# A two-layer decoder on one core: the first self attention's scores on sixteen 32x32 parts of the array, masks without scores, and a new order of steps

## The chip, the core and the metric

The kernel runs on one core of a Trainium2 chip. The core has a matrix engine (PE, with its weight loads shown apart as PEld), a vector engine (DVE), a scalar engine (ACT), a general engine (POOL) and a queue for transfers (SP). The metric is the device time of one execution in microseconds; the median of several runs is given. Traces come from one profiled execution.

## The reference

Sixteen sequences `x` of 128 tokens by 128 features pass through six residual stages; `ctx` is a context of the same shape.

```python
x = x + L0_attn(layernorm(x))          # self0: causal, 16 heads of 8
x = x + L0_xattn(layernorm(x), ctx)    # cross0: 8 heads of 64
x = x + L0_ffn(layernorm(x))           # ffn: ternary weights, rounded activations
x = x + L1_attn(layernorm(x))          # self1: causal, 16 heads of 8, scores clipped at +-10
x = x + L1_xattn(layernorm(x), ctx)    # cross1: 16 heads of 64
x = x + L1_ffn(layernorm(x))           # moe: 8 gated experts
# L0_attn, per head h:
scores = einsum('bhqd,bhkd->bhqk', q, k) * scale
scores = where(key > query, -inf, scores)
attn = softmax(scores)                 # then attn @ v and the output projection
```

## The kernel before, in words

Each sequence is one tile of 128 partitions by 128 columns. A stage is cut into steps, named stage.step: for self0 these are `rs`, `nm`, `xT`, `xTe` (layer norm and turning over), `qk`, `qke` (projection and its copies), `v`, `ve`, `vc` (values, cut in three bf16 parts), `s1` (scores), `mx.0`, `mx.1` (DVE: row maximum and difference, of eight heads each), `t.0`, `t.1` (PE: turning the differences over), `ex` (ACT: exponentials), `lo` (POOL: low part of the weights), `pv`, `at`, `oT`, `oTe`, `y`, `res`. Each step runs once for each of the sixteen sequences, written below as s1(3) for sequence 3. The keys and values of the context (`cross0.k`, `cross1.v` and so on) don't depend on `x` and are made ahead. The steps named `hi` and `lo` of a weight (`e_k.hi` on ACT, `e_k.lo` and `m_w.lo` on POOL) cut it once into a high and a low part.

`ORDER` (line 209) holds one string for each engine: two letters for a step, and the next sequence each time the step comes again. Every engine runs its string as written, and waits on semaphores where a step needs another engine's. The `Plan` class walks the strings with the durations given in `all_steps` (line 82, the entry of `self0.s1` is on line 114) and picks PSUM banks; the banks of two heads' groups (S) are pairs of the eight banks, the smaller fills (X) take one.

`self0.s1` (line 1217) makes the scores of all 16 heads in four PSUM banks, four heads to a bank. Partition is the query, column is head and key. First it writes the causal mask, -1e30 where key > query, with 16 bf16 matmuls on 32x32 parts of the array (line 1228): stationary a 32x32 part of an identity, moving a mask tile repeated over four heads, 512 columns. The four mask tiles hold the mask with its rows turned by 0, 32, 64 and 96 partitions, so each of the sixteen pairs of row part r and query part b finds its rows. Then `quarters` (line 1240) adds the scores with four fp32 matmuls on 32x128 parts (line 1244): 32 rows (four heads' features) of the queries as stationary, the keys of four heads as moving, each head in its own rows and zeros in the others' (`by_head`). `self1.s2` uses `quarters` alone. Going from one division of the array to another is counted by the plan (`array_parts`, `switch`).

At the end, with no more sequences to fill in, PE runs `keep_busy`: matmuls of a mask that nobody reads, one ahead of the last `moe.g` and four ahead of the last `moe.gT`. After that `moe.gT` turns the gate weights over, ACT copies them (`gTe`), and the last `moe.b` adds parts of the experts and biases.

Of the kernel before, what the change touches and what calls it, by code (L numbers as in the profile page):

```python
# [14 lines left out]
P = 128  # L15
NSEQ = 16
# [65 lines left out]
def all_steps():  # L82
# [22 lines left out]
    def self_attention(L, source, maxima, following, loads, loads_out):  # L105
# [8 lines left out]
        add(f"{L}.{first}", "PE", 1240 if maxima else 875, [f"{L}.qke"], [f"{L}.pv"], "S", turns)  # L114
# [52 lines left out]
    for name, load, engine, hi, lo in (("ctx0", "c0", "DVE", 530, 610), ("b_k", "b_k", "DVE", 530, 610),  # L167
# [42 lines left out]
    PE=(  # L210
        "aHaJa4a4aOa4aLa6a4aHa6aQaJa6aUa6bYbqbWbWbYbWaXaObYaLb2b2aZaUbYb0aHaQaJb0b0b0a1a6aXaObaa4aLaHbcaJaZaQ"
        "bea1aUa6b2a4b0a4aXaObabWaLbjbcaUaHblaZaQaJbebnbWa1aXbYbWaOaZbwa4a1aLa4bab2bcbybjaHaUbeblbCaQbGbEbabn"
        "bYaJaXbcbJaZaLb2bja1bebwblaHa6bya4a6bQaObCa6bEbna6baaUbSbjbcbUbGaQbJblb6bebwb8bybnccb0aXbCcabQaLaJbE"
        "claZaHbGbSbUa1chbjbJcjblb6bacqb8bwcabycccla4bncsbQaOb2bWaJbcbSaQa6bCcubUbEaUchbWbwcvbybeb6cqcaaXbJcs"
        "aZb8aLbGaHcza1clcccja4cCcDcubjcvbQb2aObCaJa4bSblcHbaaUa6czbcbUbEbncCaQchbeb6bGcDbJaXcacLb8cqaLbwcHcl"
        "cjcsccbQcuaZaHbycva1bWbYbSbjbUaOblbaaJbYbCbcaUbEcLczbnaQbWcCcqcDbGchb6bebJcscjbwcaaXb8cHbyclccaZa4a1"
        "bQcua6bjaLaHcvaObCaJblbEb0aQbGbnbaczbSaUcqcCbUbcchbJcsbeaXcLbwb6cDcaaZb8a1bycHclcjccbQbWb2cucLcvbSbj"
        "bUaLaOblbCb0babEbnaQczaHbcbGaUcCcDaJb6cqb8bebJcsaXchcaaLbwcccjaZbyclaHa1cua6cvbja4bQaOblbScHa4aJbnba"
        "aQczbcaUbCcCcqbUbEcDcLchbebJcscjaXb6bGbWb8aZcacHaLa1ccclbwcubyaHcvbjbYbQaOblbSbCb2bUbEbaaQbccLbnchb6"
        "aUczb8bGcCcabebJcjbYcDcqccclcsaXcucHbwcvaZbybQaJbjaLb0b0a1blaObCa6aHbEbna6bSaQcLbYczaJbUbGbaaUcCchcD"  # L220
        "bccqb6bwbebJaXcab8cjcsccaZaLbyclcHcua1aHcvbjbYb0aOblbQb2bnbaaUbcczaQchcCaJcqbSbeaXbUcLcDcscjaOaZb6b0"
        "bCcab8bGa1aLaQbEccaUbwclbjbybYcuaXcvblbJaZb2babncHczbccqa1cCbecsbCcLcDbYbabQbcbGcHchbSbEcLbUbjcjbJbe"
        "blcub6bwcvb8bycabWccczbnclbQcDbjb2bSbWcCbCbUblbEchbncqbJb6cjbwcabGb8byclcscccubQcvb0b2bWbScHbCbWczbw"
        "bEcLbGcCbUchcDbycjbJb6cqb8cacsccclbCcucvbEb0bQbJbGbSbYbUchb2cHczcjb6bYcCcacqb8clcsbQcccLbSb0bUcucDcv"
        "b6b2b8cacqchccczcjclcscCcDcHb2cub0cvchcLcqcjcHczcscCcucLcvcDczcHcCcLcDcHcL"
    ),
    DVE=(
        "aEarataEavaPaEaTaEbpbraYaTaPa2aEaYaPaTbfaEa2bhaYaTaPaEbfboa2aYbubhbxa2aTbzaPbfaEbobhaYbubKbNbfbxa2bz"
        "bhbRaTboaPbVbubKbNbxbfbzbocdbhaYcfbRcmaEbVa2cobubNbKbxbzcdcmbocfbRaPbuaTaEbVcobxcwbzbfaYbKbNbhcmcBa2"
        "cdcEcocGcJcwbRaTcfaPbVcEcBbocGbfaEbubKbNcMcJaEbhbxcmaYcdbRbzcwa2cobVaTaPcfcMcBbocEcGcJbubfbNbKbhbxaY"  # L230
        "bzcmcda2bRcocfcwaPaTboaEcEcBbVbucGbKbNbfaYcMbxcJbha2cmbzcdbRcocMcwcfbVaPaTcBbocEaEcGcJbubfbNbKbhaYbx"
        "cdbzcma2cfcwcobRaPaTbocBcEbVcGcMcJbfbKaEbNaYbhbua2cdbxcmbzcwcfbRaPbVaTboaEcMcocEcBcGbfbNbKbhbucJcdcm"
        "aYbxcwbzbRcfa2coaPboaTbVcMcBcEbucGcJbxbfbNaYbKbhcdbzcma2cwcfcoaTaPbRbocBcEcGbfbVaYcMbucJbhaPaTa2cdbx"
        "cmbzcfaYcwcobKbNbocBa2cEbfcGcMbhbRcJbVbubNbKbfbxcwbzcMbhcdbocBcmbRcfcocEbVcGcJbobubKbNbxbzcmbucdbRcw"
        "cfcocBbxcEcMbVcGcJbzbNbKcdcmcwcfbRbKbVcobNcBcEcGcmbRcdbVcocfcMcwcJcdcBcmcfcEcocwcGcMcJcBcEcGcwcMcJcE"
# [13 lines left out]
        "aRcicFbTcraKbtbgb5ctckbBb7a0b1bDcbbHb9bvaMaRbFaVcebkcna9bZbBbma0cybbb3bLcAbdcIcrbOcFa9bgctbbbZbDbtcI"
        "bHbdbTcibFbkb5ckbObvbLb7bgb9cybmbXcbcAbBcecnbkbTbXbDb3cFbmbFcibtb5crbvb7bLcbbObtb9bHckctcncebvbBb1b3"  # L250
# [1280 lines left out]
```

## Time and profile before

| | us |
|---|---|
| median of 3 runs | 499.54 (499.09 to 501.29) |
| the profiled execution | 499.82 |
| its span, first to last instruction | 498.1 |
| PE busy | 489.5 |
| ACT busy | 436.5 |
| DVE busy | 399.9 |
| POOL busy | 370.7 |

The span lies inside the device time; 1.7 us of the profiled execution lie around it. Busy time is the union of an engine's instructions; the ends of matmuls are modelled, and successive ones overlap, so the distance from start to start says more of PE than the sum of durations.

### The profile page before, as it was taken

What the parts mean: (1) busy time and instruction counts of PE and PEld (TensorE: products, weight loads), DVE (VectorE), ACT (ScalarE), POOL (GpSimd) and SP (SyncE); (2) the same over time, 40 slices, a digit from 0 to 9 for tenths busy, and PEclk for the clock granted to TensorE, in tenths of its full rate; (3) what the DMA queues carried; (4) which work ended last, traced back from release to release, by engine and by line L of the source; (5) the groups of instructions that cost most, each with busy time, mean ns of one, the idle gap of its engine ahead of it and who ended that gap; (6) DMA issues with size and microseconds to landing.
All of it is one profiled execution on the core that took longest, in us unless ns stands there. A gap on an engine that the chain in (4) does not pass through costs nothing.

```text
span 498.1 us, 15720 instructions
## 1 busy us (share of the span) xinstructions
PE 489.5 (98%) x5514; PEld 417.4 (84%) x5514; DVE 399.9 (80%) x906; ACT 436.5 (88%) x1180; POOL 370.7 (74%) x455
## 2 busy tenths in 40 slices
PE   8999999999999999999999999999999999999997
PEld 4778887888888888889889888888888898988885
DVE  5767778897888888989898898878898687866765
ACT  5988889999998898998898898989789899989782
POOL 2876677797868887788768886976869688568754
PEclk9999999999999999999999999999999999999999
DMA  6900000000000000000000000000000000000000
GB/s 194 338 2 1 3 2 2 1 2 2 2 3 1 7 2 9 1 3 7 7 3 1 8 3 5 4 7 1 4 7 1 8 7 3 7 3 2 7 7 16
DMA packets 6460, 8.64 MB, mean 17 GB/s; under 512 B 1392, under 2 KB 4848, under 8 KB 6384
## 3 DMA queue, kind: packets, MB, share of 16 engines
q1 hardware_dynamic: 5952, 6.86, 4.1%
q8 instruction: 45, 0.74, 0.6%
q10 hardware_dynamic: 432, 0.79, 0.4%
q14 instruction: 31, 0.25, 0.2%
HBM read 6.50 MB, written 1.05 MB: 15 GB/s over the span
## 4 chain that ended last, share of the span: by engine, by line
PE 90%; ACT 4%; DVE 2%; SPq 1%; DMA 1%; issue 1%; POOL 1%; DVEq 0%; POOLq 0%; ACTq 0%
PE psum L1270 14%; PE psum L1257 10%; PE psum L1297 10%; PE psum L1213 8%; PE psum L1335 8%; PE psum L1244 6%; PE psum L1283 3%; PE psum L1463 3%; PE psum L1347 3%; PE psum L1308 2%; PE psum L1285 2%; PE psum L1316 2%; PE psum L1310 2%; PE psum L1317 2%; PE psum L1318 2%; PE psum L1309 2%
## 5 line engine op out<-in xcount | busy, mean ns | idle before, releaser
L723 POOL TENSOR_TENSOR w_self<-w_self 128x1024 f16<-128x1024 f32 x64 | 121.1, 1899 | 27.5 <-ACT w_self L794 13.8
L805 ACT ACTIVATE w_cross<-psum,row_max_cross 128x128 f32<-128x128 f32 x384 | 104.1, 408 | 5.6 <-DVE row_max_cross L980 4.6
L728 POOL TENSOR_TENSOR w_cross<-w_cross,e_rec_cross 128x1024 f32<-128x1024 f32 x48 | 90.9, 1897 | 20.6 <-DVE e_rec_cross L989 20.6
L980 DVE TENSOR_REDUCE row_max_cross<-psum 128x8 f32<-128x1024 f32 x48 | 57.9, 1214 | 13.6 <-PE psum L1257 13.0
L987 DVE TENSOR_REDUCE e_sum_cross<-w_cross 128x8 f32<-128x1024 f32 x48 | 58.2, 1213 | 4.4 <-ACT w_cross L805 4.2
L1257 PE MATMUL psum<-kT_cross,qT_cross 64*128 64x128 f32 x768 | 54.4, 283 | 0.0
L1297 PEld LDWEIGHTS psum<-w_cross,v_cross 128*64 128x64 f32 x768 | 41.1, 136 | 14.3 <-issue 11.0
L813 ACT ACTIVATE w_cross<-psum 128x1024 f32<-128x1024 f32 x48 | 49.9, 1042 | 3.4 <-PE psum L1270 3.2
L1257 PEld LDWEIGHTS psum<-kT_cross,qT_cross 64*128 64x128 f32 x768 | 46.3, 187 | 6.8 <-issue 4.9
L1297 PE MATMUL psum<-w_cross,v_cross 128*64 128x128 f32 x768 | 51.4, 278 | 0.3 <-ACT w_cross L813 0.3
L1270 PE MATMUL psum<-ident,w_cross 128*128 128x128 f32 x384 | 49.8, 274 | 0.1
L1270 PEld LDWEIGHTS psum<-ident,w_cross 128*128 128x128 f32 x384 | 43.1, 142 | 1.4 <-ACT by_head_self L770 0.3
L998 DVE TENSOR_TENSOR w_self<-psum,row_max_self 128x1024 f32<-128x1024 f32 x32 | 39.2, 1225 | 2.4
L996 DVE TENSOR_REDUCE row_max_self<-psum 128x8 f32<-128x1024 f32 x32 | 38.9, 1215 | 1.3 <-PE psum L1244 1.0
L1007 DVE SCALAR_TENSOR_TENSOR w_self<-psum,s_bound 128x1024 f32<-128x1024 f32 x32 | 37.8, 1215 | 2.5 <-PE psum L1244 2.4
L788 ACT ACTIVATE w_self<-w_self,shift 128x1024 f32<-128x1024 f32 x32 | 36.9, 1160 | 2.4 <-DVE w_self L1007 2.4
L770 ACT ACTIVATE by_head_self<-psum,head_mask 128x128 f32<-128x128 f32 x128 | 37.2, 403 | 0.0
L794 ACT ACTIVATE w_self<-psum 128x1024 f32<-128x1024 f32 x32 | 33.1, 1035 | 4.1 <-PE psum L1270 3.5
L1244 PE MATMUL psum<-by_head_self,plain_self 32*128 32x512 f32 x256 | 36.5, 639 | 0.2
L770 ACT ACTIVATE attnT_cross<-psum 128x512 f32<-128x512 f32 x48 | 29.7, 621 | 6.9 <-PE psum L1297 6.3
L1335 PE MATMUL psum<-e_o,attnT_cross 128*128 128x128 f32 x256 | 34.3, 277 | 0.0
L1270 PE MATMUL psum<-ident,w_self 128*128 128x128 f32 x256 | 33.5, 274 | 0.4 <-DVE w_self L998 0.4
(213 smaller groups left out, 1377.5 us busy)
## 6 DMA issues: line engine op xcount, KB each, us to landing
out_dram<-x_all SPq DMA_DIRECT2D x16, 64.0 KB, 1.6
x_all<-in_x SPq DMA_DIRECT2D x1, 768.0 KB, 7.6
cT_all<-in_ctx SPq DMA_DIRECT2D x1, 768.0 KB, 9.8
e_k<-in_e_k SPq DMA_DIRECT2D x1, 512.0 KB, 5.4
e_v<-in_e_v SPq DMA_DIRECT2D x1, 512.0 KB, 6.2
e_q<-in_e_q SPq DMA_DIRECT2D x1, 512.0 KB, 8.4
e_o<-in_e_o SPq DMA_DIRECT2D x1, 512.0 KB, 9.6
m_w<-in_m_w SPq DMA_DIRECT2D x1, 512.0 KB, 8.2
```

The lines of the kernel that those rows point to most:

```text
L723: pool.tensor_tensor(L.w_low[u], L.w[u][:], halves(L.w[u][:]), ALU.subtract)\
L728: pool.tensor_tensor(L.diff[u][:].rearrange("p (h k) -> p h k", h=UNIT), L.e[u][:].rearrange("p (h k) -> p h k", h=UNIT), L.e_rec[:, u, :] ...
L770: act.activation(dst, src, ACT.Copy, **scale).then_inc(emptied(i, name)[0], 1)
L805: last = act.activation(L.e[u][:, P * p:P * (p + 1)], S_[:, P * p:P * (p + 1)], ACT.Exp, bias=L.row_max[:, u, p:p + 1])
L813: act.activation(L.w[u][:], group(i, turn)[:], ACT.Copy).then_inc(taken(i, turn)[0], 1)
L980: dve.tensor_reduce(L.row_max[:, u, :], group(i, turn)[:].rearrange("p (h k) -> p h k", h=UNIT), AX_X, ALU.max, negate=True).then_inc(L.ma ...
L987: dve.tensor_reduce(L.e_sum[:, u, :], L.e[u][:].rearrange("p (h k) -> p h k", h=UNIT), AX_X, ALU.add)
L1244: last = pe.matmul(group(i, name, u)[:, 512 * half:512 * (half + 1)], L.plain[rows, :], L.by_head[rows, :, :].rearrange("p j n -> p (j n)" ...
L1257: last = pe.matmul(S_[:, at:at + P], L.qT[rows, h // 2, :], kT[rows, h // 2, i % 2, :], start=True, stop=True)
L1270: last = pe.transpose(S_[:, P * k:P * (k + 1)], L.diff[u][:, P * k:P * (k + 1)], ident[:])
L1297: last = pe.matmul(bank(i, name)[rows, P * pair:P * (pair + 1)], v[:, h, :], L.w[c][:, P * place(h):P * (place(h) + 1)], start=True, stop= ...
L1335: last = pe.matmul(bank(i, y)[:, 0:P], L.attnT[:, k, :], L.o_w[:, k, :], start=k == 0 and not with_x, stop=k == 4 * L.chunks - 1)
```

## The change

The step `self0.s1` makes its scores by 16 fp32 matmuls, one for each pair of row part r (four heads, a bank of its own) and query part b (32 queries), over the keys 0 to 32(b + 1) - 1 of each of its four heads. Keys behind that get the mask alone, by 12 bf16 matmuls (three query parts, four row parts), and the block of 32 keys on the diagonal gets the mask added by 16 more. All of them are on 32x32 parts. `self1.s2` keeps its quarters. The plan's entry for the step goes from 1240 to 980 and the step is taken to leave the array in 32x32 parts. The strings of PE, DVE, ACT and POOL are new orders of the same steps; SP's is the same. The four `keep_busy` matmuls ahead of the last `moe.gT` are gone.

```diff
-        add(f"{L}.{first}", "PE", 1240 if maxima else 875, [f"{L}.qke"], [f"{L}.pv"], "S", turns)
+        add(f"{L}.{first}", "PE", 980 if maxima else 875, [f"{L}.qke"], [f"{L}.pv"], "S", turns)
...
 ORDER = dict(
     PE=(
-        "aHaJa4a4aOa4aLa6a4aHa6aQaJa6aUa6bYbqbWbWbYbWaXaObYaLb2b2aZaUbYb0aHaQaJb0b0b0a1a6aXaObaa4aLaHbcaJaZaQ"
+        "aHaJa4a4aOa4aLa4a6aHaQa6a6a6aUaJbqbYbYbWbWbWaXaObYaLb2aZb2aUb0bYaHaQb0aJa1b0b0a6aXaOaLbaa4aHbcaZaJaQ"
...
     if step == "s1" and L == "self0":
-        return "32 by 32", "32 rows"
+        return "32 by 32", "32 by 32"
...
                     pe.wait_ge(masks_turned, 16 * 6)
-                for j in range(4):
-                    for b in range(4):
-                        queries, r = slice(32 * b, 32 * (b + 1)), (b + j) % 4
-                        rows = slice(32 * r, 32 * (r + 1))
-                        pe.matmul(group(i, name, j // 2)[queries, 512 * (j % 2):512 * (j % 2 + 1)]
-                                  .rearrange("p (h k) -> p h k", h=4),
-                                  ident_b[rows, rows], mask[j][rows, :].unsqueeze(1).broadcast_to([32, 4, P]),
+                def rows(r):
+                    return slice(32 * r, 32 * (r + 1))
+
+                def scores(r, b, keys):
+                    half = group(i, name, r // 2)[rows(b), 512 * (r % 2):512 * (r % 2 + 1)]
+                    return half.rearrange("p (h k) -> p h k", h=4)[:, :, keys]
+
+                def masked(r, b, keys, stop):
+                    keys_of = mask[(r - b) % 4][rows(r), keys]
+                    n = keys.stop - keys.start
+                    return pe.matmul(scores(r, b, keys), ident_b[rows(r), rows(r)],
+                                     keys_of.unsqueeze(1).broadcast_to([32, 4, n]), start=False, stop=stop)
+
+                for b in (3, 2, 1, 0):
+                    for r in range(4):
+                        keys = slice(0, 32 * (b + 1))
+                        pe.matmul(scores(r, b, keys), L.plain[rows(r), rows(b)], L.by_head[rows(r), :, keys],
                                   start=True, stop=False)
-                quarters(L, i, name, False)
+                for b in range(3):
+                    for r in range(4):
+                        masked(r, b, slice(32 * (b + 1), P), False)
+                for b in range(4):
+                    for r in range(4):
+                        last = masked(r, b, rows(b), True)
+                last.then_inc(s_full, 1)
...
                 if step == "gT":
                     room(i, name)
-                    if i == NSEQ - 1:
-                        keep_busy(bank(i, name), 4)
```

## Rows read from the trace of the kernel before

**Rows 1.** Profile page, part 1: busy us (share of span) and instructions.
```profile
PE 489.5 (98%) x5514; PEld 417.4 (84%) x5514; DVE 399.9 (80%) x906; ACT 436.5 (88%) x1180; POOL 370.7 (74%) x455
```
**Rows 2.** Profile page, part 4: chain that ended last, share by engine.
```profile
PE 90%; ACT 4%; DVE 2%; SPq 1%; DMA 1%; issue 1%; POOL 1%; DVEq 0%; POOLq 0%; ACTq 0%
```
**Rows 3.** By stage: us, busy PE, PEld, DVE, ACT, POOL, clock, DMA share, GB/s.
```profile
0.00:25.00 25.00, 22.22 (x190) 15.85 (x191) 16.04 (x52) 18.24 (x37) 13.38 (x21) 1.00 0.76 265
25.00:125.00 100.00, 98.31 (x1135) 81.77 (x1134) 78.37 (x156) 91.30 (x241) 73.54 (x92) 1.00 0.01 2
125.00:425.00 300.00, 300.00 (x3514) 261.41 (x3510) 256.49 (x576) 270.77 (x744) 240.03 (x292) 1.00 0.02 4
425.00:475.00 50.00, 49.48 (x543) 43.01 (x543) 34.90 (x77) 43.98 (x125) 32.77 (x39) 1.00 0.02 5
475.00:498.10 23.10, 19.51 (x147) 15.38 (x141) 14.15 (x48) 12.21 (x38) 10.95 (x13) 1.00 0.04 12
```
**Rows 4.** Timeline, PE, one self0.s1: start us, busy us, line, operands, shapes, count.
```profile
209.48 0.43 PE L1228 MATMUL psum<-mask,ident_b 32*32 32x512 bf16 x16
209.84 1.14 PE L1244 MATMUL psum<-by_head_self,plain_self 32*128 32x512 f32 x8
210.92 0.33 PE L1463 MATMUL psum<-ident,xn_self 128*128 128x128 f32 x1
```
**Rows 5.** The same timeline, its window cut at 209.88 us.
```profile
209.84 0.71 PE L1244 MATMUL psum<-by_head_self,plain_self 32*128 32x512 f32 x4
```
**Rows 6.** Line 1228: count, duration ns min/median/max, first and last start us.
```profile
L1228 PE MATMUL psum<-mask,ident_b x256: 371/385/386, 9.0 to 364.6; 32*32 32x512 bf16 x128
```
**Rows 7.** Chain of waits in order of time: start us, us, engine, line, records.
```profile
378.82 1.02 PE psum L1297 x16
...
415.37 0.89 PE psum L1335 x8
```
**Rows 8.** Timeline, PE, one-pass records of 512 columns in a row.
```profile
487.91 0.40 PE L1428 MATMUL psum<-m_w_lo,moe_hi 128*128 128x512 f32 x1
...
488.14 0.39 PE L1429 MATMUL psum<-m_w_hi,moe_hi 128*128 128x512 f32 x1
```
**Rows 9.** Timelines of PE and POOL early, and line 618 on POOL.
```profile
18.17 0.36 PE L1308 MATMUL psum<-cT_hi,e_k_lo 128*128 128x256 f32 x1 [0.38 <-POOL e_k_lo L618]
...
40.44 0.40 POOL L713 TENSOR_TENSOR v_self<-v_self 128x128 f32<-128x128 f32 x1 [4.21 <-ACT v_self L770]
...
L618 POOL TENSOR_TENSOR m_w_lo<-m_w,m_w_hi x1: 2364/2364/2364, 123.8 to 123.8; 128x1024 fp32r<-128x1024 f32 x1
```
**Rows 10.** Timeline of the end, all engines.
```profile
491.43 0.47 PE L1427 MATMUL psum<-m_w_hi,moe_lo 128*128 128x512 f32 x1 [0.51 <-DVE moe_lo L965]
...
492.65 0.22 DVE L1076 TENSOR_SCALAR g_weight<-psum,g_rec 128x8 f32<-128x8 f32 x1
...
492.89 1.04 PE L1456 MATMUL psum<-mask,ident_b 128*128 128x512 bf16 x4
493.17 0.62 ACT L823 ACTIVATE attnT_cross<-psum,g_mix 128x128 f32<-128x128 f32 x2 [1.66 <-PE psum L1429]
...
493.77 0.27 PE L1436 MATMUL psum<-ident,g_weight 128*128 128x128 f32 x1
494.08 0.28 ACT L770 ACTIVATE g_weightT<-psum 128x128 f32<-128x128 f32 x1 [0.28 <-PE psum L1436]
...
494.41 0.71 PE L1445 MATMUL psum<-attnT_cross,ident 128*128 128x128 f32 x4 [0.37 <-ACT g_weightT L770]
...
495.83 0.29 DVE L1104 TENSOR_TENSOR x_all<-psum,xn_moe 128x128 f32<-128x128 f32 x1 [0.61 <-PE psum L1445]
```

More of the change, by code:

```diff
@@ new lines @@
+        "bea1aUb2a4a4a6b0aXaOaLbWbabjbcaUblaZaHaQaJbea1bnbWaXbWbYaOaZa4bwa4bab2aLbca1bjbyaHaUbeblbCaQbnbGbabY"
+        "bEaJaXbcbJaZaLb2bja1beblbwa4aHbya6a6bQaOa6bCbnbEa6baaUbjbSbcbGbUaQbJblb6bebwb8bybnccb0aJaXaLcabCbQbE"
+        "aZclbGaHa1bSbUchbjbJcjblb6bacqb8bwcabycccla4bncsbQaObWbSb2aJa6bcaQcubUaUcvbCchbwbEbeb6bWbycqcaaXbJcs"
+        "aZb8aLbGaHcza1clcccja4cCcDbjcub2bQcvaObabSaJa4bCblcHaUbca6czbUbEbncCaQchbeb6bGcDbJaXcacLb8cqbwcHaLcl"
+        "cjcsccbQcubyaZaHcvbWbSa1bjbYbUaOblbabYaJbcbCaUczbEbnaQcCcqbWcLcDchbGb6bebJcjcsbwcHcabyaXb8clccaZa4a1"
@@ new lines @@
+        "bQaLa6cubjaHcvaObCaJblbEb0bSaQbnbGbaczaUbUcqcCbcchbJcsbeb6aXcLcDcabwcHaZb8bya1clcjccbQcuaLbWcLbSbjcv"
+        "b2bUaOblbCb0bEbabnaQbcaHczaUaJcCbGcDb6cqb8bebJcsaXchcabwcccjaZbyclaLa1cua6cvaHa4bjbQaOblbaa4aJbnaQbS"
+        "bcbCczaUcHbUcCbEcqcLcDchbebJcjcsaXb6bGbWb8aZcaa1bwaLccclcHcubyaHcvbjbYbQaOblbCbSb2bUbEbaaQbcbncLchcz"
+        "b6aUb8bGcCcabebJcjbYcDcqccclcsaXcubwcHcvbyaZaJbQbjaLa1b0b0blaObCbSa6bEbnaHa6aQbGbYczbUcLaJbaaUcCbccD"
+        "chcqbwb6bebJaXcab8cscjccaZaLbyclcHcua1cvaHbjbYb0aOblbQb2bnbaaUbcczaQchaJcCcqbSbeaXbUcLcDcscjaOb6bCb0"
@@ new lines @@
+        "bzcmcda2bRcocfcwaPaTbocBbVcEbuaEcGbNbKbfcMaYcJbxbha2cmbzcdbRcocMcfcwbVaPaTbocBcEcGcJbuaEbfbNbKbhaYbx"
+        "cdbzcma2cfcwcobRaPaTbocBcEbVcGcMcJbubfbNbKaYbha2bxcdcmbzcwcfbRaPbVaTbococMaEcEcBcGbfbNbKbubhcJcdcmaY"
+        "bxaEcwbzbRa2cfcoaPboaTbVcBbucEcMcGcJbxbfbNbKbhaYcdbzcma2cwcfcoaTaPbRbocBcEcGbfbVcMaYcJbhaPbuaTa2cdbx"
+        "cmbzcfaYcwcobKbNbocBa2cEbfcGcMbhbRcJbubVbNbKbfbxcwbzbhcdcBbocmbRcMcfcEcocGbVcJbobubKbNbxbzcmbucdbRcw"
+        "cfcobxcBcEcMbVcGcJbzbNbKcdcmcwcfbRbKbVcocBbNcEcGcmbRcdbVcocfcwcMcJcdcmcBcfcocwcEcMcGcJcBcEcGcwcMcJcE"
@@ L249 @@
[L249 to L252 removed]
+        "aGaqasaIaKaua5aGa5a5a5a7aMawaIaRayaVaKa7a7bZa7bZbXbXbXaAbZaGb3b3aCaMaVb1aIa0aRaKbZb1a7b1b1aGa9aMbbaI"
@@ L257 @@
[L257 to L260 removed]
+        "apaFaFaNaxaSaWaFazaBaNaWaSaFa8aFaNaDa3aSaWa8biaFaNa3aWaSbsa8biaFa8bAaNaWaSa3bsbibIaFbMbPa3bAa8bibsaW"
@@ new lines @@
+        "b4aNaSbMbAbIbPbsbicgbIa3b4a8cpbPaFbMaNbscgaFbAaSb4cpaWa3bAcxbMbIbia8bPcpcKa3cxcgaWb4aNbsaSaFbMbPbIbi"
+        "bAcxa8b4cpaNcKcgbsaSaWbIaFbPbMbibAa8cKcxaNcpa3cgbsb4aSaWbMbPbIbicKbAcpa8cxb4aFcga3bsaWa3aSaNbIaFcKbP"
+        "bMbia8cxbAcgcpaSbsa3aWb4aNbPbIbia8bMcxbAaNcgb4cKbsa3aFbIaScpaWbMbibPcKbAcxa8cgaNbscpb4aSaFa3aWcKbibP"
+        "bMa8bAbIaNcpcxcgaWaSbsb4a3cKbibIaSaNaWbAa8cgcxcpbMa8a3bPbsbib4bIcKbPcxbAbMa3bibscgcpb4cKbsbMbPbIbAcx"
+        "cgb4cpbAcKbPbIbMcxcgb4bIcpbMbPb4cpcgcxcKcgcpcxcKcxcKcK"
@@ L1237, in self_scores2 @@
                 room(i, name)
-                quarters(L, i, name, True)
-            def quarters(L, i, name, start):
                 for u in range(2):
@@ L1244, in quarters @@
                         last = pe.matmul(group(i, name, u)[:, 512 * half:512 * (half + 1)], L.plain[rows, :],
-                                         L.by_head[rows, :, :].rearrange("p j n -> p (j n)"), start=start, stop=True)
+                                         L.by_head[rows, :, :].rearrange("p j n -> p (j n)"), start=True, stop=True)
                 last.then_inc(s_full, 1)
```

60 lines of the change are left out of this document (20 added, 40 removed).

## The prediction

> **What bounds the kernel now.** I read the busy shares first [rows 1]: PE 98% of the span, ACT 88%, DVE 80%, POOL 74%. A busy PE is not PE at its peak, so I asked next what ends the span. The chain of waits is 90% PE [rows 2]. The table by stage [rows 3] says where PE has holes: 2.78 us in the first 25 us, 1.69 us from 25 to 125, none in the 300 us from 125 to 425, 0.52 us up to 475 and 3.59 us in the last 23 us. The granted clock is 1.00, the 2.4 GHz level, in every stage. So PE is one packed queue, and a nanosecond of its slots taken out of the middle comes off the end, until another engine is late. The nearest is ACT: 91.30 of 100 us between 25 and 125, 90% from 125 to 425 [rows 3]. Taking 1% off PE's time lifts that to 91 or 92%, still under PE.
>
> The step that changes is self0.s1, sixteen times. One of them [rows 4]: sixteen masks start at 209.48, eight score records at 209.84, the next step at 210.92. The slot, first start to next start, is 0.36 + 1.08 = 1.44 us. PE waits for nothing in it, and sixteen slots (the 256 masks, from 9.0 to 364.6 us, are sixteen times sixteen [rows 6]) are 23.0 us. That is what the change can work on.
>
> **Prices of the parts.** A score matmul of 512 fp32 columns is two records: the eight are four row parts times two, and the first four start together and make a busy stretch of only 0.71 us when the window cuts them from the rest [rows 5]. So passes of different array parts run side by side: first passes of all parts, then second passes. Eight fp32 records of 128 columns one behind the other take 0.89 us [rows 7], 0.111 each, so 512 columns in two records are 8 x 0.111 = 0.89 us. One-pass records of 512 columns start 0.23 us apart [rows 8]; I use that for a bf16 mask of 512 columns, and 0.06 for 128. What is left of a slot is the cost of entering and emptying one division of the array: 1.08 - 0.89 = 0.19 for the quarters, whose four weight loads are 128 columns wide, and 0.36 - 0.23 = 0.13 for the 32 by 32 masks. Sixteen masks of 0.385 each [rows 6] cover 0.43 [rows 4], so sixteen starts cost about 0.05, and sixteen bf16 streams do run at once.
>
> **The new slot.** Removed: sixteen masks of 512 columns (0.23), the change of division between masks and quarters, and the score columns of keys behind a part's last query. Added: 16 score matmuls on 32x32 parts of 128, 256, 384 and 512 columns for the query parts b = 0 to 3, 12 masks of 384, 256 and 128 columns for b = 0 to 2, and 16 diagonal masks of 128. All of it is in one division, entered once (0.13). The longest part is b = 3: 0.89 of scores and 0.06 of diagonal mask. If the shorter parts finish their scores and masks under it, the slot is 0.89 + 0.06 + 0.13 = **1.08 us**, the floor. If instead no mask gets going until the longest scores are through, b = 0 then has 384 + 128 mask columns left: 0.89 + 0.23 + 0.13 = **1.25 us**. No row of before has parts of unequal length, so I cannot say which; both ends rest on equally near rows and I take the middle, 1.165. Saving per slot 0.275 (0.19 to 0.36), times sixteen **4.4 us** (3.0 to 5.8). (The table entries 1240 and 980 in the diff are the order's assumptions; no term uses them.)
>
> Here the Trainium skill can be set beside the rows. The rows show starts in program order but only equal lengths. "TensorE: Matmul & The Clock Gate", Part 3, The mechanism, says that matmuls keep program order in their start and also in their end. By that rule a short part's score, issued later, ends no earlier than the long one, and the slot is the upper end: 16 x 0.19 = 3.0 us saved in place of 4.4. I keep it as the upper end, since no row here shows it.
>
> **What of it reaches the end.** Fifteen of the sixteen are followed by PE work without a hole of consequence. The first is not: behind it PE waits 0.38 us at 18.17 for POOL's e_k_lo [rows 9], so its 0.3 is lost (the new order puts e_k.lo one POOL step and e_k.hi one ACT step earlier, which may give it back; I count the loss). Sum so far 4.4 - 0.3 = 4.1.
>
> **The order.** By the two strings, 417 of 737 PE steps keep their place, the mean shift is 0.75 places and the largest 9; all sixteen self0.s1 stand where they stood; the changes of array division are 190 before and 189 after. DVE keeps 270 of 405, ACT 299 of 679, POOL 82 of 277, SP all. Most moves swap neighbours and I cost them at zero; what hides them is the steps held ready ahead of PE (keys and values of the context). If that cover is gone, a swap is a wait of the size now seen, 0.4 to 0.7 us. The one large move is m_w.lo on POOL, 52 places earlier, behind self0.vc(2). It is 2.364 us long [rows 9] and issues nothing else; behind it queue self0.bi(0) and both lo of sequence 2, and for these self0.pv(2) on PE and s1(3). Its cover is POOL's 4.21 us idle at 40.44, where it waits for v of sequence 2 [rows 9]; PE and ACT take that v earlier in the new order, so the subtraction fits. Without the cover it costs up to 2.4 us once. For the order as a whole: it can win at most the holes, 2.2 us between 25 and 475, and I take zero.
>
> **The end.** The change drops four filler matmuls ahead of the last moe.gT. They start at 492.89 and occupy PE until gT at 493.77, though its input was made by 492.87 [rows 10]. gT is what ACT's copy at 494.08 waits for, and the last ten records wait for that copy. ACT's own two parts before it end at 493.79 [rows 10], so the copy can come 0.29 earlier: gain 0.3. Against it, PE then idles up to 1 us there; should its clock fall to the 1.2 GHz level, the ten records from 494.41 until the DVE step at 495.83 double at worst, and the edit costs 1.1. The nearest row, PE's hole of 0.51 ahead of the last moe.e [rows 10] with the clock still at 1.00 after it [rows 3], speaks for no fall; I take a gain of 0.2, ends -0.3 and +1.1.
>
> **Sum.** -4.1 - 0.2 = -4.3 us. The profiled run took 499.82 with a span of 498.1 (1.7 lies around it), so it would become 495.5 and 493.8; the median of the runs is 499.54, so the forecast is **495.2 us**.
>
> **Rivals.** (a) The gain turns into waits: slots end at other times than the order assumes, and PE meets an ACT copy or a POOL subtraction that isn't done. If each of the sixteen slots brings a wait of 0.2, half of the hole of 0.38 seen early, 3.2 of 4.3 are gone: 498.4. For it: ACT at 91% early, thousands of small moves of place. Against: 300 us without a hole now.
> (b) The change doesn't do what it says: score passes go four parts at a time, as in the rows, not sixteen. Then the second pass of a group holds up the next: at the prices above the passes start at 0, 0.44, 0.78, 1.00 and 1.11, the last ends at 1.22, the masks of b = 0 add 0.23, and the slot is 1.45 + 0.13 = 1.58. Sixteen times +0.14, less 0.2: 501.6. The rows show groups of four only because four parts exist; two 64-column parts go by two, sixteen records in 1.02 [rows 7].
> (c) Slower: four fp32 streams of one row part don't run at once. All four column parts of a row part read the same SBUF rows of by_head. If they queue, 128 x (1 + 2 + 3 + 4) = 1280 columns in place of 512 are 2.23 us, the slot is 2.42 and the sum +15.7: 515. It decides from the point where these scores take over 1.25 us, that is, under 1.8 streams at once. Against it: bf16 streams ran sixteen at once [rows 6], and fp32 by two column parts [rows 7]; no row has four.
> (d) Stepped outputs. Scores and masks now write four runs of 32 to 96 columns with gaps in each bank; every output of before is in one run. If that halves the rate, the slot is 2 x 0.95 + 0.13 = 2.03, sixteen times +0.59, 509. The Trainium skill, "PSUM — Partial Sum Buffer", Specifications (TRN2), says that any non-contiguous access pattern slows matmuls significantly; no row here shows one, and runs of 32 are long, so it gets a small chance.
> (e) Better: the floor of 1.08 with a hole or two closed: 492.4.
>
> **How the numbers follow.** Forecast 0.64, (a) 0.15, (b) 0.07, (c) 0.05, (d) 0.05, (e) 0.04. The range 492.4 to 499.0 holds the forecast with both ends of its slot, most of (a) and (e), about 0.8. A run of this kernel can be told from no change from about 0.5%, 2.5 us. Faster by more than that (under 497.0): most of the forecast, (e) and a third of (a), 0.73. Within: the rest of (a), (b) and the forecast's weak end, 0.17. Slower: (c) and (d), 0.10.
>
> **What would show it.** In the profile after, the slot from the first score record of a self0.s1 to the next step: 1.08 to 1.25 us by the forecast, 1.6 by (b), over 2 by (c) and (d). In a cut window sixteen first passes start within 0.1 us, four by (b). The masks for b = 0 start before the last second pass ends if the floor holds, after it if the upper end does. PE's holes per stage should stay near the table; more than 3 us more between 25 and 475 is (a). The last ten records keep 0.11 us apart and the clock 1.00. What would make the prediction wrong above all is a new slot that is no shorter, since everything else in the sum is under half a microsecond.

## The result, and the profile after

| | median us | range, runs | ratio to before, 95% interval |
|---|---|---|---|
| before, its runs beside after | 499.73 | 499.09 to 501.29, 19 | |
| after | 502.01 | 500.30 to 502.56, 19 | 1.0034 [1.0025, 1.0043] |

The forecast was 495.2 us, faster. The change made the kernel slower, by 0.3%. The profiled execution of after took 500.77 us with a span of 499.0; 0.9 us of span were added to the 498.1 of before. (The runs of most kernels here fall at two levels about 1.6 us apart, those of after 12 times of 19 at the upper one and those of before 3 times of 19; where that comes from is part of the experiments.)

The page's shares and chain answer [rows 1] and [rows 2]:

```profile
PE 488.5 (98%) x6086; PEld 420.9 (84%) x6086; DVE 400.5 (80%) x906; ACT 438.5 (88%) x1180; POOL 371.3 (74%) x455
...
PE 82%; ACT 5%; POOL 4%; issue 4%; POOLq 2%; DVE 2%; DMA 1%; DVEq 0%; ACTq 0%
```

PE has 572 records more (6086 against 5514), is busy 1.0 us less, and the chain that ended last leaves it more often: 82% in place of 90%. By stage (columns as in [rows 3]: stretch, us, busy time of PE, PEld, DVE, ACT, POOL, granted clock, DMA share, GB/s):

```profile
0.00:25.00 25.00, 21.33 (x264) 16.37 (x265) 15.93 (x52) 18.60 (x37) 12.69 (x20) 1.00 0.79 265
25.00:125.00 100.00, 98.09 (x1293) 82.81 (x1293) 78.34 (x158) 91.62 (x241) 75.98 (x93) 1.00 0.01 2
125.00:425.00 300.00, 299.82 (x3846) 262.82 (x3847) 256.27 (x570) 270.87 (x740) 237.79 (x290) 1.00 0.02 4
425.00:475.00 50.00, 49.66 (x541) 42.90 (x543) 34.92 (x80) 44.13 (x122) 33.86 (x41) 1.00 0.02 5
475.00:498.10 23.10, 19.59 (x158) 16.00 (x155) 15.04 (x49) 13.27 (x43) 10.96 (x13) 1.00 0.04 11
```

The hole at the start is 3.67 us where [rows 3] had 2.78; in the other stages the busy time of PE is within 0.3 us of before (the last row stops at 498.10, 0.9 us short of this span). So nothing was won in the middle. One self0.s1 in the timeline of PE says why (start us, busy us, line, operands, shape of the first, count), to be laid beside [rows 4]:

```profile
182.00 1.06 PE L1244 MATMUL psum<-by_head_self,plain_self 32*32 32x512 f32 x32
182.64 0.87 PE L1238 MATMUL psum<-mask,ident_b 32*32 32x384 bf16 x28
183.44 0.66 PE L1314 MATMUL psum<-w_cross,v_cross 128*64 128x128 f32 x8
```

From 182.00 to 183.44 is the new slot: 1.44 us, as before. All sixteen measure 1.426 to 1.440 us and sum to 22.99 us, against 22.99 before. The same timeline with its window cut at 182.10, then run from 182.60 to 183.00 and from 183.05 to 183.45, shows what happens inside:

```profile
182.00 0.63 PE L1244 MATMUL psum<-by_head_self,plain_self 32*32 32x512 f32 x16
...
182.64 0.32 PE L1238 MATMUL psum<-mask,ident_b 32*32 32x384 bf16 x1
...
183.07 0.44 PE L1238 MATMUL psum<-mask,ident_b 32*32 32x384 bf16 x27
```

and PEld's timeline has the weight loads of the masks in the same slot:

```profile
182.21 0.09 PEld L1238 LDWEIGHTS psum<-mask,ident_b 32*32 32x32 bf16 x1
182.64 0.09 PEld L1238 LDWEIGHTS psum<-mask,ident_b 32*32 32x32 bf16 x1 [0.34 <-issue]
183.07 0.30 PEld L1238 LDWEIGHTS psum<-mask,ident_b 32*32 32x32 bf16 x26 [0.34 <-issue]
```

Sixteen first passes start within 0.10 us, so sixteen fp32 streams do run at once. Then nothing of the masks starts, though parts fall idle one after the other. One mask starts at 182.64, the other 27 not before 183.07. By the single records, in ns from the slot's start: first passes 0 to 100; second passes at 215 to 235 for b = 0, at 296 for b = 1, 375 for b = 2, 456 for b = 3, though they were issued in the opposite order; the first score record of b = 3 ends at 613 and the first mask starts at 640; the first b = 3 score is through with its second record at 1043, and 27 masks start from 1070 on, 8.3 ns apart in the mean, the last at 1286, each right behind its weight load; the next step starts at 1440.

At the end (PE and DVE; [rows 10] has the same of before) the four fillers are gone:

```profile
494.35 0.30 PE L1451 MATMUL psum<-ident,g_weight 128*128 128x128 f32 x1
495.36 0.71 PE L1460 MATMUL psum<-attnT_cross,ident 128*128 128x128 f32 x4 [0.70 <-ACT g_weightT L770]
...
496.77 0.29 DVE L1104 TENSOR_TENSOR x_all<-psum,xn_moe 128x128 f32<-128x128 f32 x1 [0.22 <-PE psum L1460]
```

From the start of gT to the start of the last DVE step 2.42 us pass; in [rows 10], from the first filler at 492.89, 2.94.

### The profile page after: what moved, and what is told of

The parts are those of the page before. It is cut to its first block, busy times and chain, and to the rows that moved or that the text cites. A ratio compares the mean times of both kernels' runs of the same rounds, so it can differ in the third digit from the quotient of the medians.

```text
span 499.0 us, 16866 instructions
## 1 busy us (share of the span) xinstructions
PE 488.5 (98%) x6086; PEld 420.9 (84%) x6086; DVE 400.5 (80%) x906; ACT 438.5 (88%) x1180; POOL 371.3 (74%) x455
## 4 chain that ended last, share of the span: by engine, by line
PE 82%; ACT 5%; POOL 4%; issue 4%; POOLq 2%; DVE 2%; DMA 1%; DVEq 0%; ACTq 0%
PE psum L1287 13%; PE psum L1314 9%; PE psum L1274 8%; PE psum L1213 8%; PE psum L1352 7%; PE psum L1261 3%; PE psum L1300 3%; PE psum L1244 3%; PE psum L1364 2%; PE psum L1478 2%; POOL w_cross L728 2%; PE psum L1325 2%; ACT w_cross L805 2%; PE psum L1327 2%; PE psum L1326 2%
## 5 line engine op out<-in xcount | busy, mean ns | idle before, releaser
L1213 PE MATMUL psum<-xnT_cross,e_q 128*128 128x128 f32 x256 | 33.4, 277 | 0.2 <-ACT xnT_cross L770 0.2
```

What stands on the lines that cost most here:

```text
L1213: last = pe.matmul(bank(i, name)[:, P * k:P * (k + 1)], w[:, col:col + P], xT, start=True, stop=True)
```

## Experiments

The theory of the slot, formed from the records above: **a PE instruction enters only while fewer than 64 lie between it and the oldest one that isn't through.** Each fp32 score counts four (two weight loads, two matmuls), each mask two. Sixteen scores are 64. So the masks stand outside until the oldest score, b = 3, is through, whatever part they are for. The single loads fit: when the oldest score's first weight load is done, one place is free, and the load of the first mask enters alone (182.21, as the second pass on its part begins); when its first record ends at 182.61 two more are, and that mask's matmul and the next mask's load enter (182.64). Rivals: that a mask waits for the type (fp32 to bf16) to change on the whole array; that the order, the missing fillers or the body made the time by other ways.

**Body alone, order alone.** The diff of the first: the new `self_scores1` in the kernel before, with its order and its fillers. The second: the new strings (of which one line is shown, and the plan's 980) with the body of before and the fillers.

```diff
-                for j in range(4):
...
+                for b in (3, 2, 1, 0):
...
-        "aHaJa4a4aOa4aLa6a4aHa6aQaJa6aUa6bYbqbWbWbYbWaXaObYaLb2b2aZaUbYb0aHaQaJb0b0b0a1a6aXaObaa4aLaHbcaJaZaQ"
+        "aHaJa4a4aOa4aLa4a6aHaQa6a6a6aUaJbqbYbYbWbWbWaXaObYaLb2aZb2aUb0bYaHaQb0aJa1b0b0a6aXaOaLbaa4aHbcaZaJaQ"
...
```

> The order, the plan's entries and the fillers of before; only the body of self0.s1 is the change's (16 scores, longest part first, then 28 masks). Theory, entry window: the slot is 1.44 us as in the profile of the changed kernel, because masks that stand behind 64 PE instructions (16 scores of two weight loads and two matmuls each) begin only when the oldest score has ended; so the body gives nothing and the time is that of before, 499.7 within 0.6 us. Rival, the new order is what eats a gain of the body: with the order of before the slots are shorter or the holes fewer and the time is near 495.

> The new order and plan entries, with the body of before and with the four fillers ahead of the last moe.gT. Theory: the order assumes slots 0.26 us shorter than they are, meets waits for it, and is by itself about 1.2 us slower than before: 500.9, with all runs at one level. Rival, the order is neutral and the loss lies in the body: 499.7.

Measured: body alone 500.88 us median (499.81 to 501.75, 12 runs), ratio 1.0017 [1.0004, 1.0029], slots 1.427 to 1.450 us. Order alone 500.06 (499.84 to 501.81, 11 runs), 1.0011 [1.0002, 1.0020], slots 1.435 to 1.440. So the body gives nothing in either order, and the new order costs about 0.4 us. That is less than the 1.2 us I expected of the order, and its runs aren't all at one level (one is at 501.81). Six of the body's twelve runs lie near 500.0 and six near 501.6; its lower level is itself some 0.4 us above that of before.

**The fillers.** The changed kernel with the four `keep_busy` matmuls back (the diff); and the kernel before without the same two lines.

```diff
                     room(i, name)
+                    if i == NSEQ - 1:
+                        keep_busy(bank(i, name), 4)
```

> The changed kernel with the four fillers ahead of the last moe.gT put back. Theory, the end: without them the granted clock falls in the last microseconds of most runs; with them it stays at 1.00 in all runs, the level near 502 is gone and all runs lie near 500.8 (the lower level of 500.4 and 0.4 for the fillers). Rival, the two levels come from waits of the new order: they remain, near 500.8 and 502.4.

> The kernel before without the four fillers ahead of the last moe.gT, nothing else. Theory, the end: the last copy starts 0.3 to 0.4 us earlier where the clock holds, and where it falls the last matmuls take up to 1.3 us more: two levels, near 499.3 and 501.0. Rival, the fillers only occupy PE: one level near 499.3.

Measured: with the fillers back 500.94 us (500.72 to 502.58, 8 runs), 1.0034 [1.0021, 1.0047], still at two levels, so these don't come from the fillers' absence; that part of my theory fell. Without the fillers the kernel before took 499.41 (498.77 to 500.83, 12 runs), 0.9997 [0.9988, 1.0006]: not told from no change by its runs, but in its trace the ACT copy starts at 493.69 in place of 494.08 [rows 10] and the last DVE step at 495.44 in place of 495.83.

**Short scores first.** If the oldest instruction holds the door, the order of the scores sets when masks enter. With b = 0 first the oldest leaves early.

```diff
-                for b in (3, 2, 1, 0):
+                for b in (0, 1, 2, 3):
```

> As e1_body_only, with one line turned: the scores of the shortest part go first and those of the longest last (b = 0, 1, 2, 3). Theory, entry window: a PE instruction begins only when fewer than 64 stand between it and the oldest unfinished one; with the short parts oldest, eight masks enter at about 0.43 us, eight more and again eight as the next parts end, and only the last four wait for the longest scores at about 1.12 us. The slot falls to 1.30 us (1.26 to 1.34) and the time, 16 x 0.13 less, to about 497.8. Rival, type change: bf16 masks wait until every fp32 pass has drained; the slot stays 1.44 and the time that of e1_body_only.

Measured: 499.37 us (498.26 to 500.24, 12 runs), 0.9986 [0.9973, 0.9998], slot 1.317. One line of order took 0.12 us off the slot. The time that I had forecast from it, 497.8, wasn't reached: six runs lie near 498.5 and six near 500.1. The timeline of PE:

```profile
238.45 0.71 PE L1240 MATMUL psum<-by_head_self,plain_self 32*32 32x128 f32 x24
238.77 0.32 PE L1234 MATMUL psum<-mask,ident_b 32*32 32x384 bf16 x1
...
238.88 0.35 PE L1234 MATMUL psum<-mask,ident_b 32*32 32x384 bf16 x7
...
239.14 0.69 PE L1234 MATMUL psum<-mask,ident_b 32*32 32x128 bf16 x20
239.77 0.33 PE L1313 MATMUL psum<-w_cross,v_cross 128*64 128x128 f32 x2
```

One mask at 0.32 us, seven from 0.43, twenty from 0.69, while fp32 scores still run. bf16 masks beside fp32 scores refute the change of type. By the single records the twenty are nine from 0.69, eight from 0.91 and three from 1.15: groups of 1, 7, 9, 8 and 3, which is what the count of 64 gives if each score returns its places when all before it are through.

**Twelve scores.** The body of after in the order of before, with the scores of b = 0 left out, so that part of the computation is missing. 48 of 64 places are then taken by scores and eight masks should enter at once.

```diff
-                for b in (3, 2, 1, 0):
+                for b in (3, 2, 1):
```

> As e1_body_only, with the four score matmuls of query part b = 0 left out (its masks take their place alone), so that part of the computation is missing. Theory, entry window: twelve scores are 48 instructions, so eight masks, at two each, fill the 64 and start before the first score record ends at 0.61 us; one more starts as it ends, and the other nineteen after the oldest score's second record at about 1.04 us. Rival, type change: no mask starts before 1.0 us.

Measured (one run, 498.99 us; slot 1.371), the timeline of PE with its window cut at 237.30, run from 237.80 to 238.00 and from 238.26:

```profile
237.29 0.34 PE L1234 MATMUL psum<-mask,ident_b 32*32 32x384 bf16 x4
...
237.72 0.40 PE L1234 MATMUL psum<-mask,ident_b 32*32 32x256 bf16 x5
...
238.28 0.37 PE L1234 MATMUL psum<-mask,ident_b 32*32 32x128 bf16 x19
```

Eight are in: four at 0.08 us and four at 0.51, of 256 columns, for b = 1. The ninth starts at 0.70 us from the slot's start, after the oldest score's first record, and 19 at 1.07. Eight, one, nineteen: 48 + 2 x 8 = 64, the number of the theory. In every run here an fp32 score has twice the instructions of a mask, so a window of 32 matmuls with one weight load let in ahead would give the same groups; no run tells the two apart.

**Masks first.** Sixteen full masks of 512 columns, which need two places each and wait for nothing, then the sixteen scores, with both orders of steps.

```diff
+                for b in (3, 2, 1, 0):
+                    for r in range(4):
+                        pe.matmul(scores(r, b, slice(0, P)), ident_b[rows(r), rows(r)],
+                                  mask[(r - b) % 4][rows(r), :].unsqueeze(1).broadcast_to([32, 4, P]),
+                                  start=True, stop=False)
                 for b in (3, 2, 1, 0):
                     for r in range(4):
                         keys = slice(0, 32 * (b + 1))
```

> The order, plan entries and fillers of before; the body first writes the sixteen whole masks of before, part by part, and then adds sixteen scores over the keys each query part can see, longest first. Theory, entry window: behind the oldest unfinished score stand at most 60 instructions, so nothing is kept out; the longest part sets the slot, 0.03 to load, 0.21 of mask, 0.85 of scores, 0.02 of starts, 0.09 to empty: 1.20 us, and the time is 16 x 0.24 = 3.8 us less, about 495.9. Rival, type change: fp32 waits for all bf16 masks to drain, 1.33 us and 498.0. Rival, the order of before makes nothing of shorter slots: 499.7.

> The body of e6_masks_first in the changed kernel, with its order and plan entries and the four fillers put back. Theory: slots of 1.20 us are what the new order was searched for (980 and 196 in its table make 1.18), so it gets the 3.8 us and doesn't lose the 0.4 that it lost with the body of before: about 495.5, no slower than e6_masks_first. Rival, the new order is worse by itself by 0.4 us or more whatever the slots are: 496.3 or above and slower than e6_masks_first.

Measured: with the order of before 498.76 us (498.19 to 499.99, 12 runs), 0.9982 [0.9970, 0.9993]; with the order of after and the fillers 498.97 (498.25 to 502.03, 12 runs), 0.9991 [0.9973, 1.0010]. The slot is 1.184 us where nothing holds the next step, the middle of what the prediction had for the change itself. With the new order 495.5 was expected, and the two orders can't be told apart here. PE's timeline:

```profile
238.18 0.43 PE L1233 MATMUL psum<-mask,ident_b 32*32 32x512 bf16 x16
238.40 1.03 PE L1239 MATMUL psum<-by_head_self,plain_self 32*32 32x512 f32 x32
239.36 0.41 PE L1306 MATMUL psum<-w_cross,v_cross 128*64 128x128 f32 x2
```

But the time was to be 495.9. Laying the start of every step beside that of the same step in before: the sixteen slots are 3.88 us shorter together (19.12 against 22.99); the first of them starts 1.65 us late; and between the slots 1.90 us come back, 0.05 to 0.24 at a time but for the first, though the steps there are the same and in the same order. Part of that is visible in the last line: the two records of the 64-column parts span 0.41 us where before the same two span 0.33 (239.10 us there), as the second of them starts 95 ns after the first where before it was 7 (the longest scores, b = 3, hold only one half of the columns, which is the likely reason); five of the sixteen slots are followed by this step, 0.4 us in all. The rest needed a run of its own.

**What a slot at the floor is worth.** The kernel before with the masks left out (it no longer hides later keys), so that the slot becomes that of self1.s2.

```diff
-                for j in range(4):
...
-                quarters(L, i, name, False)
+                quarters(L, i, name, True)
```

> The kernel before with the masks of the first self attention left out (so its output is not the reference's), the eight score records of 512 columns kept: its slot becomes that of the second self attention, 1.07 us in place of 1.436, which is the floor of 1.08 that the forecast gave. It asks what the forecast's slot would have been worth at the end. If all of it reaches the end, 16 x 0.365 = 5.8 us: 493.8. Theory (masks first showed some 0.1 us of each slot's gain given back in the next step, where PE now meets ACT's copies that it had met just done): about two thirds reach the end, 3.9 us: 495.7, with the lag against before falling by less than 0.365 from one slot to the next. Rival: ACT binds and under a third reaches the end: 497.9 or more.

Measured: 497.55 us (497.35 to 497.87, 6 runs), 0.9950 [0.9935, 0.9966], against 499.85 of its runs of before. The slot is 1.071 us where nothing follows late; the sixteen are 5.22 us shorter, and 2.3 us reach the end. My two thirds were too much; it lies closer to the rival. 2.66 us come back between the slots. The chain of waits through one such place (start us, us, what):

```profile
291.46 0.67 ACT w_cross L805 x2
292.13 0.38 ACT xn_self L832
292.51 0.50 ACT kT_cross L770
293.01 0.04 issue
293.05 0.50 PE psum L1308
```

and the timelines of PE at the same step, of the run without masks and then of before:

```profile
292.72 0.27 PE L1455 MATMUL psum<-ident,xn_self 128*128 128x128 f32 x1
293.05 0.50 PE L1308 MATMUL psum<-e_v_hi,cT_all_lo 128*128 128x512 f32 x1
```

```profile
294.72 0.27 PE L1463 MATMUL psum<-ident,xn_self 128*128 128x128 f32 x1
294.75 0.47 PE L1316 MATMUL psum<-e_v_hi,cT_all_lo 128*128 128x512 f32 x1
```

Before, the two start 0.03 us apart; without masks 0.33, and the chain runs through ACT: exponentials, xn_self, the copy of kT_cross, and only with that copy done the context's values. ACT had started this stretch 0.50 us ahead of the slot in both runs, on work that PE made before it, so a shorter slot doesn't bring it forward. PE comes early and stands. This place gives back 0.3 of the 2.66 us. Laying the 5258 records of PE in this run beside those of before, one by one, shows that others wait for DVE: the largest single return, 0.62 us at 25.29, stands behind DVE's attn_self, and at six places PE's turning of w_self (t) starts 0.04 us after DVE's differences of the same scores (mx) are done, 0.12 to 0.28 us later than its place in before would give, 1.2 us together.

**The start, and the two levels.** Two more executions of the changed kernel, profiled:

> The changed kernel itself, looked at again. Theory (start): if this run is over 501.3 us, the first records of cross0.k.0 stand 0.21 us apart until 10 us; if it is under 501.0, 0.12. Rival: a run over 501.3 with these records 0.12 apart.

> The same as the run before it: over 501.3 us with records of cross0.k.0 0.21 us apart, or under 501.0 with 0.12, by the theory of the start.

Measured: 500.25 us and 502.19. PE's timeline at the first self0.qk and in cross0.k.0, of the one and of the other, and the start of the other (nine matmuls that nobody reads):

```profile
6.90 0.68 PE L1364 MATMUL psum<-xnT_self,a_qk 128*128 128x128 f32 x4 [0.69 <-ACT xnT_self L770]
...
7.66 0.28 PE L1326 MATMUL psum<-cT_all_lo,b_k_hi 128*128 128x256 f32 x1
7.77 0.29 PE L1327 MATMUL psum<-cT_hi,b_k_hi 128*128 128x256 f32 x1
```

```profile
1.88 4.02 PE L1497 MATMUL psum<-weighted 128*128 128x512 bf16 x9 [1.88 <-DVE weighted L1184]
...
7.11 1.20 PE L1364 MATMUL psum<-xnT_self,a_qk 128*128 128x128 f32 x4 [0.94 <-ACT xnT_self L770]
...
8.32 0.41 PE L1326 MATMUL psum<-cT_all_lo,b_k_hi 128*128 128x256 f32 x1
8.53 0.41 PE L1327 MATMUL psum<-cT_hi,b_k_hi 128*128 128x256 f32 x1
```

Records of 256 columns stand 0.21 us apart in place of 0.12: half rate, the 1.2 GHz level. The table by stage prints 1.00 there, but it only subtracts what the trace lists, and the first entry of the trace's list of granted clocks, with 1.00, starts at 10.79 us in the second run and at 6.75 in the first. The nine matmuls from 1.88 us on stand 0.43 apart, half rate as well. So the clock hadn't fallen in PE's hole, as an expectation below has it; it had not risen yet. The second run enters its first self0.s1 1.75 us later than the first, its last 1.90, of 1.94 us between their times: nearly all of the step between the levels is made in the first 11 us. The three other profiles of upper-level runs (the body alone, short first, masks first with the order of before) have this half rate too, and where their traces list the clock it reads 1.00 from 10.44 (short first) and 10.35 us (masks first) on; after, the fillers back, masks first with the new order, all of the lower level, and the twelve scores (one run) have not. In all other profiles that list it, the clock is up by 4.6 to 7.5 us.

What leaves PE idle there: ACT's timeline at the start, of before and then of after.

```profile
5.43 0.63 ACT L843 ACTIVATE b_k_hi<-b_k 128x512 fp32r<-128x512 f32 x1
6.16 0.28 ACT L770 ACTIVATE xnT_self<-psum 128x128 f32<-128x128 f32 x1
```

```profile
6.11 0.63 ACT L843 ACTIVATE b_k_hi<-b_k 128x512 fp32r<-128x512 f32 x1 [0.39 <-DMA b_k<-in_b_k]
6.64 0.26 ACT L770 ACTIVATE xnT_self<-psum 128x128 f32<-128x128 f32 x1
```

The first loads of ctx and b_k land 4.2 and 4.9 us after their issue in place of 3.5 and 4.2; ACT's copy of xnT_self stands behind b_k_hi and is 0.5 us later, and PE waits 1.59 us for it where it waited 0.46. The rest of that longer wait is no loss: in this execution of after the clock was up at 4.58 us, the nine matmuls took 3.43 us in place of the 4.02 of before, and PE reached the wait earlier:

```profile
1.88 3.43 PE L1497 MATMUL psum<-weighted 128*128 128x512 bf16 x9 [1.88 <-DVE weighted L1184]
...
7.05 0.68 PE L1364 MATMUL psum<-xnT_self,a_qk 128*128 128x128 f32 x4 [1.59 <-ACT xnT_self L770]
```

The later landing goes with the body and not with the order: 4.3 and 4.9 us in the body alone and in masks first, 3.5 and 4.3 in the order alone, 3.7 and 4.3 without masks. The issues are the same in all. The programs differ in one more row of the DMA queues: those with late loads fetch 48 to 50 packets of instructions on one queue, those with early loads 43 to 45. Whether this is why they land later stays open, and so does whether the later loads keep the clock down longer.

I tried twice to fill the hole with three matmuls of 512 columns on zeros, in the changed kernel, behind and then ahead of the wait for the load of a_qk, and once in masks first without the fillers at the end (behind that wait). The diff is of the second:

```diff
                 if step == "qk":
+                    if i == 0 and L is self0:
+                        room(i, name)
+                        for _ in range(3):
+                            pe.matmul(bank(i, name), still[:, 0:P], still[:, 0:512], start=True, stop=True)
```

> The changed kernel with one thing added: three matmuls of 512 bf16 columns on zeros between PE's first transposition (5.16 us in its trace) and the first self0.qk (7.05 us), where PE idles 1.59 us waiting for ACT's copy. Theory (start): the changed kernel's runs lie at two levels, about 500.5 and 502.1 us, because its early loads land some 0.4 us later, PE idles longer there, and in some executions the granted clock has fallen when the first cross0.k starts, whose records are then 0.21 us apart where they are 0.12 us at the 2.4 GHz level. With the hole filled the upper level goes: median 500.5, at most two of twelve runs over 501.3. Rival (the upper level has another cause, such as the end): the median stays at 502.0 with half of the runs or more over 501.3. Either way the slot of self0.s1 stays 1.437 us.

> The changed kernel with three matmuls of 512 columns on zeros ahead of the first self0.qk's wait for the load of a_qk, so that they fill PE's hole from 5.2 to 7.0 us. Theory (start): the runs of the upper level are executions in which the granted clock is down when cross0.k.0 starts; with the hole filled they go: median 500.5, at most two of twelve over 501.3. Rival (the levels come from elsewhere): median 501.5 or more, half of the runs over 501.3.

> Masks first (sixteen full masks, then sixteen scores of growing or full length, the order of before), without the four fillers at the end and with the three matmuls at the start. By the theory of the start, its median is the lower level of masks first, 498.3, less the 0.3 that the fillers cost: 498.0 us, with at most two of twelve runs over 499.2; the slot 1.184 us. If the start is not the cause of the two levels, the median is 498.5 and half of the runs are near 499.3.

Measured: 502.86 us (500.91 to 504.67, 10 runs), 1.0050 [1.0030, 1.0071]; 502.67 (501.08 to 504.60, 7 runs), 1.0049 [1.0029, 1.0069]; 498.39 (498.04 to 500.36, 12 runs), 0.9966 [0.9949, 0.9983]. In the changed kernel both missed what I had forecast, a median of 500.5 with nearly all runs at the lower level. The three matmuls filled nothing; they waited for the same thing as qk, here in the second:

```profile
6.88 0.82 PE L1361 MATMUL psum<-weighted 128*128 128x512 bf16 x3 [0.88 <-ACT xnT_self L770]
...
7.90 0.36 PE L1325 MATMUL psum<-cT_hi,b_k_lo 128*128 128x256 f32 x1
```

cross0.k.0 then runs at the full rate, but starts 0.3 us later. This profiled run (502.67 us) is not one of the three at 501.1, and its loss is at the other end, where PE idles ahead of the last moe.e (two stretches, columns as in [rows 3]):

```profile
492.00:493.70 1.70, 0.86 (x4) 0.68 (x5) 1.10 (x7) 0.39 (x2) 1.56 (x2) 1.00 0.00 0
493.70:499.00 5.30, 4.20 (x15) 3.09 (x13) 2.56 (x9) 1.31 (x5) 1.14 (x3) 0.50 0.04 12
```

The granted clock is 0.50, the 1.2 GHz level, from 493.70 to the end. So the clock cost time at two places: at the start, where it rises at 10.4 to 10.8 us in some executions, and in the tail, where it fell in this one. In masks first the same three matmuls left eleven of twelve runs between 498.04 and 498.82; that version, with a ratio of 0.9966, is the fastest of those that leave nothing out, ahead of both kernels. They didn't fill the hole there either: PE starts them at 6.80 us, after 0.69 idle behind the same copy. What took the upper level away, they or another difference between the two programs, isn't told apart: it is shown where the 1.75 us are lost and at which clock, not why the clock rises late, and no cure.

## Why the prediction was wrong, point by point

**The new slot** is the step that failed. I let the slot be set by columns: 0.89 of scores, a tail of mask columns, 0.13 for entering. The scores were near enough: 1.04 us until the oldest is through. The floor supposed that masks get going as soon as their part is free; PE's entry doesn't ask for that, it counts instructions from the oldest one. The upper end supposed "no mask gets going until the longest scores are through", which is what happened to 27 of 28, but priced what follows at 512 columns, 0.23 us. It is 27 starts 8.3 ns apart, each behind a weight load that had to enter as well, and the last mask behind them: 1.070 + 0.216 + 0.154 = 1.44. From the end of the oldest score that tail is 0.40 where I had 0.23: 0.17 of the 0.19 us by which the slot passes the upper end. Sixteen savings of 0.275 became none. A row of before hinted at a part of it: sixteen masks spread over 0.05 us, a cost I wrote down and then didn't multiply. It would have given too little, since those start 3.4 ns apart: 0.09 us for 27 in place of 0.22.

Of the Trainium skill, "TensorE: Matmul & The Clock Gate", Part 3, The mechanism, the prediction took the rule that matmuls keep program order in start and end, as the upper end. In after the masks do start behind every score, but the trace contradicts the rule for passes: second passes start at 215, 296, 375 and 456 ns for b = 0 to 3, issued 3 to 0, and by their modelled ends finish in that order too. In short first masks also start at 0.32 and 0.43 us, ahead of the second pass of b = 3 (0.54), which was issued before them. What did bear on the case is the 64-deep window that the same section tells of; the eight, one and nineteen masks of the twelve scores agree with 64, counted from the oldest unfinished instruction with the weight loads.

**Rivals.** (b), (c) and (d) are out: sixteen first passes in 0.10 us, the second passes of b = 0 at 215 ns, and no slower streams into stepped outputs. From a part's first pass to its second 135, 242 and 348 ns pass for the 128, 256 and 384 columns of b = 0 to 2, which go into runs of 32, 64 and 96, and 456 for the 512 of b = 3, which are in one run: 0.83 ns for each column added, whether in steps or not. (a) priced waits at 0.2 per slot. There was no gain for them to eat, but where there is one they do: 1.90 us over 15 spaces in masks first, 0.13 each, 2.66 without masks, 0.18 each.

**"A nanosecond of its slots taken out of the middle comes off the end"** was wrong as well, and would have been had the slot come out at 1.07: of 5.22 us 2.3 arrived. I read the 300 us without a hole [rows 3] as PE being alone in the chain. They only say that its records cover each other; at the values of the context PE and ACT were both just in time, and at six turnings of w_self PE and DVE.

**The first slot** was to lose its 0.3 to e_k_lo [rows 9]; in after that wait is gone, as the order could give back, but with no shorter slot it had nothing to win.

**The order** was costed at zero; alone it cost 0.4 us, within what I named a swap without cover. m_w.lo ran under its cover: 38.12 to 40.48 us on POOL.

**The end** was costed at -0.2 and its -0.3 is about what the kernel before gained without fillers. Both its ends were seen: the ten records keep their rate in after, and in one run above they go at half rate, the clock having fallen at 493.71, behind PE's hole ahead of the last moe.e.

**The start** was not in the sum at all. Together: no gain in the slots, order +0.4, and 12 of 19 runs at the upper level where before had 3; the one such run of after that was profiled had cross0.k.0 at half rate. The levels of after are near 500.5 and 502.1, those of before 499.6 and 501.2, and the median of 502.01 is 0.9 us above before at the same level and 1.6 more for falling on the upper one. Of the 0.9 the runs account for 0.5: order +0.4, the body alone +0.4 at its lower level, the missing fillers -0.3; where the other 0.4 comes from stays open. Range and chances left too little for a slot that is no shorter, which the last paragraph named as the main danger without a time or a chance.

## What to carry to other kernels

Count PE's instructions as well as its columns: where many small matmuls of unequal length share the array, put those that end first (or wait for nothing) ahead, because here everything behind the 64th instruction waited for the oldest, not for its own part. A packed engine in the table isn't the only one in the chain: look at the steps behind the one you shorten, and at how long their inputs had been ready. And a change that touches no load can still move the start, so the first ten microseconds are compared too.

## What the runs showed of the hardware

- What PE lets in fits one count: an instruction enters when fewer than 64 stand from the oldest unfinished one on; an fp32 matmul here is four of them (two weight loads, two records), a bf16 one two. Masks came in groups of 8, 1 and 19 with twelve scores, of 1, 7, 9, 8 and 3 with the short ones first, of 1 and 27 in after, whose masks' loads came as 1, 1 and 26. (32 matmuls with one load ahead would look the same.)
- In that window second passes of short fp32 matmuls start ahead of those of longer ones issued earlier, by up to 0.24 us (215 against 456 ns).
- bf16 and fp32 matmuls run beside each other on different parts (masks at 0.43 us beside scores until 1.1 us in short first).
- Starts on 32x32 parts stood 3.4 ns apart for the sixteen bf16 masks of before, 6.7 for first passes of fp32, and 8.3 for the 27 masks that entered after the oldest score, as far apart as their weight loads.
- Outputs in four runs of 32, 64 or 96 columns with gaps took the same 0.83 ns for each added column as 512 in one run (135, 242, 348 and 456 ns from first pass to second).
- The granted clock's first entry at 1.00 stood between 4.6 and 7.5 us in executions whose first cross0.k ran at the full rate and at 10.4 to 10.8 in those where it ran at half, of one program at 6.75 and 10.79; the table by stage shows nothing of it, the distances of the records do (0.12 and 0.21 us).
- The first load of ctx landed 4.0 to 4.3 us after its issue in the programs with sixteen or twelve scores on 32x32 parts and 3.5 to 3.7 in the others, with the same issues.
